# Setup of a patch-pooling transformer tower: biases as a 97th contraction row, weights loaded ahead of the images

## The chip, the cores and the metric

One Trainium2 chip, one of its cores. The metric is the device time of one run in microseconds; the time of a kernel is the median of its runs.

## What is computed

`x` is 64 images x 12 channels x 224 x 224 in fp32. Everything after the first line works on 196 tokens of 192 features per image.

```python
pooled = x.reshape(64, 12, 14, 16, 14, 16).sum(axis=(3, 5))          # 16 x 16 patches
h = einsum('bcij,ce->bije', pooled, channel_weights).reshape(64, 196, 192)
q, k, v = split(layernorm(h) @ W_qkv + b_qkv)                         # W_qkv [192, 576]
h = h + softmax(q @ k.T / sqrt(192)) @ v
C = sum over 9 (e, r) of alpha_e * alpha_r * (mask_out(r*e) x mask_in(e))  # [768, 192]
hid = gelu(layernorm(h) @ (w_fc * C).T + b_fc * c0b)                  # w_fc [768, 192]
out = h + hid @ (w_proj * C.T).T + b_proj * c1b
```

## The kernel before

Every token of the first stage is a combination of 12 channel sums, so the kernel keeps tokens in a basis of at most 26 rows and folds the weights into small matrices once, in a **setup**: `sel_gram` (variance of the first norm), `score_mat` (q and k in one matrix), the basis and its centred transpose `basis_t`, `g2` (variance of the second norm), `resid` (the residual's rows), `f_rows` (w_fc in the basis) and `w1_hi`, `w1_lo` (w_proj in two fp32r parts). Then 16 **groups** of 4 images are worked through in a software pipeline.

*Image loads.* A group is 3 tiles of 128 partitions; a tile is 7 runs of 448 KB, each a DMA of its own on SyncE's (SP's) queue. `xs` holds 2 tiles (RING). VectorE sums a tile in 3 chunks of 2, 2 and 3 runs (`reduce_chunk(n, c)`, L385; c is 0 to 8 within group n). The load of a chunk waits until the chunk two tiles earlier is summed: `sp.wait_ge(reduced, PER_TILE * (tile - RING) + chunk + 1)`. So chunk (0,6), the first of tile 2, waits for sum (0,0), (0,7) for (0,1), (0,8) for (0,2), and (1,0) for (0,3).

*Order.* Each engine runs its program in order. In the groups, tables written by hand (`PE_ORDER`, `DVE_ORDER` ...) give each operation a step; they are not changed. The setup stands ahead of them. On TensorE it is one function: rows of the channel weights, Gram rows, q and k (`PE_QKT`), the score matrix (`PE_A`), coefficients (`PE_COEF`), w_fc turned (`PE_W0T`), basis and residual rows in one signal (`PE_BASIS`), the centred basis turned (`PE_BT`), g2's products, f's products, w_proj turned (`PE_W1`). `sum_rows(0)`, the first product of group 0, comes behind all of it. On VectorE the steps alternate with the first chunk sums:

```python
setup_centre(); setup_mix(); setup_gram()
reduce_chunk(0, 0); setup_scores()
reduce_chunk(0, 1); setup_biases()
reduce_chunk(0, 2); setup_basis()
reduce_chunk(0, 3); setup_g2()
```

*Biases.* q and k's, v's and w_fc's biases are added by products of their own with one contraction row: a bias row of 1 partition against a row of `cr` that has ones where wanted. For w_fc's, TensorE makes the sums c0b with two 384-wide products of 9 rows and VectorE multiplies them into `bfc_sb` in `setup_biases`. An fp32 product is two weight loads and two matmul instructions in the trace, all at line 510 (the helper `mm`); 96 is half of the 192 features (E2).

Of the kernel before, what the change touches and what calls it, by code (L numbers as in the profile page):

```python
# [163 lines left out]
def build(nc, x, cw, wqkv, bqkv, wfc, bfc, wproj, bproj, alpha_e, alpha_r, const_full, const_rows, const_paired, out):  # L164
    with ExitStack() as ctx:
# [208 lines left out]
        def _(dve):  # L374
# [75 lines left out]
            def setup_scores():  # L450
                dve.wait_ge(setup_pe, PE_A)
                dve.tensor_tensor(score_mat[:], ps[:, 1, 0:128], cf[:, MASK_S:MASK_S + 128],
                                  ALU.mult).then_inc(setup_dve, 1)

            def setup_biases():
                dve.wait_ge(setup_pe, PE_W0T)
                dve.wait_ge(wfc_landed, 32)
# [50 lines left out]
        def _(pe):  # L508
# [503 lines left out]
```

## Time and profile before

| | us |
|---|---|
| median of 3 runs | 511.71 (511.31 to 513.15) |
| profiled execution, its own time | 510.34 |
| its span, first to last instruction | 508.2 |
| busy: TensorE products / VectorE / ScalarE / GpSimd | 449.9 / 382.3 / 284.4 / 253.3 |
| first product of group 0 (`sum_rows`) starts | 58.28 |
| last chunk sum starts | 438.38 |

The granted TensorE clock is full (2.4 GHz level) throughout. 166.66 MB are moved, 156.29 of them read. In the trace, PE is TensorE, DVE VectorE, ACT ScalarE, POOL GpSimd, SPq SyncE's DMA queue. A busy share tells how full an engine is, not what sets the end; for that the waits and the order in time have to be read.

### The profile page before, as it was taken

Reading aid. Unit: us, or ns where it says so; the run is one execution under the profiler, and the core shown is the slowest. Engines: PE = TensorE matmul, PEld = TensorE weight load, DVE = VectorE, ACT = ScalarE, POOL = GpSimd, SP = SyncE. Lnnn points to the kernel's source line nnn. Section 1 sums busy time; section 2 is a strip of 40 time slices with the busy share of each in tenths; the row PEclk is TensorE's granted clock in tenths of the full one; section 3 lists DMA queues with packets and bytes.
Section 4 is the critical chain, followed back from the end, with each engine's and each line's share of the span. In section 5 each row is a group of like instructions: output and inputs, shape, how many; then the busy total and the mean of one; then the engine's idle time right before and its main releaser. Section 6 shows DMA issues by size and latency. Waiting matters only on the chain.

```text
span 508.2 us, 11125 instructions
## 1 busy us (share of the span) xinstructions
PE 449.9 (89%) x4676; PEld 374.7 (74%) x4676; DVE 382.3 (75%) x289; ACT 284.4 (56%) x461; POOL 253.3 (50%) x180
## 2 busy tenths in 40 slices
PE   4988563769999999999999999999999998999996
PEld 4644341448888888888888888888788887888886
DVE  2136979999798989898989898989899998710000
ACT  1020210363767676757575757576757575768551
POOL 1022301156283838383747474747474737475570
PEclk9999999999999999999999999999999999999999
DMA  8955999999999999999999999999999999300101
GB/s 243 347 231 194 357 390 366 395 374 397 350 372 393 401 404 401 400 401 401 401 405 401 402 400 400 403 399 400 401 400 397 402 402 390 120 25 26 49 25 49
DMA packets 56652, 166.66 MB, mean 328 GB/s; under 512 B 5967, under 2 KB 13020, under 8 KB 56602
## 3 DMA queue, kind: packets, MB, share of 16 engines
q1 hardware_dynamic: 56602, 165.95, 85.8%
q8 instruction: 37, 0.61, 0.5%
q14 instruction: 13, 0.11, 0.1%
HBM read 156.29 MB, written 9.63 MB: 326 GB/s over the span
## 4 chain that ended last, share of the span: by engine, by line
PE 48%; POOL 22%; issue 12%; ACT 8%; DVE 6%; DMA 3%; SPq 1%; POOLq 0%; ACTq 0%; DVEq 0%
PE ps L510 46%; POOL h_lo L974 10%; POOL inv L953 5%; POOL inv L965 5%; DVE pooled L385 5%; ACT h_hi L885 2%; ACT h_f L876 2%; ACT L876 2%; DMA xs<-x 2%; POOL uhat_tok L967 2%; PE ps L707 1%; POOL phat_tok L958 1%; DMA alpha_sb<-alpha_r 1%; DVE neg_tok L403 0%; ACT out_sb L891 0%
## 5 line engine op out<-in xcount | busy, mean ns | idle before, releaser
L385 DVE TENSOR_REDUCE pooled<-xs 128x28 f32<-128x1792 f32 x144 | 327.5, 2321 | 6.5 <-DMA xs<-x 6.0
L974 POOL TENSOR_TENSOR h_lo<-h_f,h_hi 128x784 fp32r<-128x784 f32 x96 | 176.4, 1866 | 125.4 <-ACT h_hi L885 125.4
L510 PE MATMUL ps<-w_hi,h_hi 128*98 128x192 f32 x768 | 205.4, 267 | 0.0
L510 PE MATMUL ps<-w_lo,h_hi 128*98 128x192 f32 x768 | 194.5, 253 | 0.0
L510 PE MATMUL ps<-w_hi,h_lo 128*98 128x192 f32 x768 | 193.9, 252 | 0.0
L510 PEld LDWEIGHTS ps<-w_hi,h_hi 128*98 128x98 f32 x768 | 126.3, 164 | 18.8 <-issue 15.5
L510 PEld LDWEIGHTS ps<-w_lo,h_hi 128*98 128x98 f32 x768 | 126.7, 165 | 0.0
L510 PEld LDWEIGHTS ps<-w_hi,h_lo 128*98 128x98 f32 x768 | 126.5, 165 | 0.0
L876 ACT ACTIVATE h_f<-ps 128x784 f32<-128x784 f32 x96 | 75.9, 825 | 20.0 <-PE ps L510 19.8
L885 ACT CAST h_hi<-h_f 128x784 fp32r<-128x784 f32 x96 | 81.7, 854 | 0.5
L953 POOL TENSOR_TENSOR inv<-var,minus_half 98x8 f32<-98x8 f32 x16 | 26.2, 1636 | 61.5 <-DVE var L399 61.5
L891 ACT COPY out_sb<-ps 98x384 f32<-98x384 f32 x64 | 30.7, 480 | 33.6 <-PE ps L510 33.1
L510 PE MATMUL ps<-rows_sb,f_rows 32*128 32x196 f32 x768 | 47.6, 364 | 1.7 <-ACT probs L847 1.7
L843 ACT COPY rows_sb<-ps 128x196 f32<-128x196 f32 x16 | 5.2, 322 | 61.5 <-PE ps L510 61.5
L403 DVE TENSOR_REDUCE neg_tok<-ps 98x4 f32<-98x784 f32 x32 | 29.7, 970 | 12.3 <-PE ps L510 12.3
L510 PEld LDWEIGHTS ps<-rows_sb,f_rows 32*128 32x128 f32 x768 | 32.5, 192 | 7.5 <-issue 2.7
L510 PE MATMUL ps<-rows_sb 32*98 32x196 f32 x512 | 33.1, 377 | 1.2 <-ACT rows_sb L843 0.8
L510 PE MATMUL ps<-resid,rows_sb 32*98 32x192 f32 x256 | 28.1, 338 | 1.5 <-ACT out_sb L891 1.5
L847 ACT ACTIVATE probs<-ps 98x784 f32<-98x784 f32 x32 | 24.6, 822 | 3.7 <-PE ps L510 3.5
L965 POOL TENSOR_TENSOR inv<-var,minus_half 98x8 f32<-98x8 f32 x16 | 26.2, 1641 | 0.6 <-DVE var L424 0.6
L510 PEld LDWEIGHTS ps<-rows_sb 32*98 32x98 f32 x512 | 21.2, 176 | 5.9 <-ACT rows_sb L843 1.3
L510 PEld LDWEIGHTS ps<-resid,rows_sb 32*98 32x98 f32 x256 | 20.1, 163 | 6.6 <-issue 4.4
(127 smaller groups left out, 386.3 us busy)
## 6 DMA issues: line engine op xcount, KB each, us to landing
xs<-x SPq DMA_DIRECT2D x336, 448.0 KB, 9.8
out<-out_sb SPq DMA_DIRECT2D x32, 294.0 KB
rows_sb<-wfc SPq DMA_DIRECT2D x1, 576.0 KB
out_sb<-wproj SPq DMA_DIRECT2D x1, 576.0 KB
h_f<-wqkv SPq DMA_DIRECT2D x1, 432.0 KB
cf<-const_full SPq DMA_DIRECT2D x1, 264.0 KB, 4.7
h_f<-const_paired SPq DMA_DIRECT2D x1, 153.0 KB, 5.8
cr<-const_rows SPq DMA_DIRECT2D x1, 83.2 KB
```

Of the source, the lines that this page charges most:

```text
L385: dve.tensor_reduce(pooled[:, n % 2, t, GRID * first:GRID * end].rearrange("p (i j) -> p i j", j=GRID), runs, AX.XY, ALU.add).then_inc(red ...
L403: dve.tensor_reduce(neg_tok[:, :, 2 * pair:2 * pair + 2, NEG].rearrange("p h b -> p b h"), ps[0:HALF, 2 * pair:2 * pair + 2, 0:2 * TOKENS] ...
L510: return pe.matmul(o, a, b, start=start, stop=stop, skip_group_check=shared)
L843: act.copy(phat_neg, ps[:, MB, 0:TOKENS]).then_inc(phat_neg_ready, 1)
L847: act.activation(probs[:, 2 * pair:2 * pair + 2], ps[0:HALF, 2 * pair:2 * pair + 2, 0:2 * TOKENS], ACT.Exp).then_inc(probs_ready, 1)
L876: act.activation(h_f32[:, t].rearrange("p (b n) -> p b n", b=GROUP), ps[:, 0:GROUP, TOKENS * (t % 2):TOKENS * (t % 2 + 1)], ACT.Gelu_apprx ...
L885: act.copy(h_hi[:, m % 2, t], h_f32[:, t]).then_inc(h_hi_ready, 1)
L891: act.copy(out_sb[:, b // 2, b % 2], ps[0:HALF, OB + b % 2, 0:2 * EMBED]).then_inc(out_ready, 1)
L953: pool.tensor_tensor(inv1[:], var1[:], minus_half[:], ALU.pow).then_inc(inv1_ready, 1)
L965: pool.tensor_tensor(inv2[:], var2[:], minus_half[:], ALU.pow).then_inc(inv2_ready, 1)
L967: pool.tensor_tensor(uhat_tok[:, :, :, 0:BASIS].rearrange("p h b c -> p (h b) c"), u_tok[:, m % 2, :, :, 0:BASIS].rearrange("p h b c -> p ...
L974: pool.tensor_tensor(h_lo[:, m % 2, t], h_f32[:, t], h_hi[:, m % 2, t].bitcast(F32), ALU.subtract).then_inc(h_lo_ready, 1)
```

## The change

Bias rows become row 97 (partition 96) of the first half of a contraction that has 96: b_qkv behind `wqkv_sb`, b_fc behind `w0t`, and in the stationary or moving partner a row of constants, brought there by five loads of 512 bytes (`row`). The coefficients get a 97th output row, so b_fc is multiplied together with w_fc on GpSimd, in two halves. The bias products disappear, but for b_proj's. SyncE's queue brings all constants, wqkv and wfc first, then the rows and the alphas, then images. On TensorE the basis is made right behind the score matrix and apart from the residual rows, the coefficients behind it, the centred basis and g2 ahead of w_fc, the residual rows behind it; the places in PSUM follow. On VectorE the steps get another order between the same chunk sums. Sizes of the tiles change with `E2B = E2 + 1`. Shown are declarations, loads and VectorE with what is removed, TensorE, ScalarE and GpSimd with the new lines only (the removed ones are printed above).

```diff
-mix_in = sb("mix_in", [MIXES, EMBED])
-cwt = sb("cwt", [E2, 2, 128])
-cwt_ctx = sb("cwt_ctx", [E2, 2, 128])
+mix_in = sb("mix_in", [MIXES, 2, E2B])
+cwt = sb("cwt", [E2B, 2, 128])
+cwt_ctx = sb("cwt_ctx", [E2B, 2, 128])
-qkt = sb("qkt", [E2, 4, 128])
+qkt = sb("qkt", [E2B, 4, 128])
-basis_t = sb("basis_t", [E2, 2, 128])
+basis_t = sb("basis_t", [E2B, 2, 128])
...
+    def row(out, at):
+        sp.dma_start(out, const_rows[0:1, at:at + 128]).then_inc(rows_landed, 16)
     sp.dma_start(cr[:], const_rows).then_inc(cr_landed, 16)
     sp.dma_start(cw_sb[:], cw).then_inc(cw_landed, 16)
-    for i in range(2):
-        load(0, 0, i)
     sp.dma_start(cf[:], const_full).then_inc(cf_landed, 16)
     sp.dma_start(paired_sb, const_paired).then_inc(cf_landed, 16)
+    sp.dma_start(wqkv_sb[0:E2], wqkv.rearrange("(k p) n -> p k n", k=2)).then_inc(wqkv_landed, 16)
+    sp.dma_start(wqkv_sb[E2:E2B, 0], bqkv).then_inc(wqkv_landed, 16)
+    sp.dma_start(wfc_sb, wfc.rearrange("(t p) e -> p t e", p=128)).then_inc(wfc_landed, 16)
+    row(cwt[E2:E2B, 0], ROW_ONE_P)
+    row(cwt_ctx[E2:E2B, 0], ROW_ONE_U)
+    row(qkt[E2:E2B, 2], ROW_ONE_P)
+    row(qkt[E2:E2B, 0], ROW_NEG)
+    row(basis_t[E2:E2B, 0], ROW_ONE_F)
     sp.dma_start(alpha_sb[:, 0:1], alpha_e).then_inc(mix_landed, 16)
     sp.dma_start(alpha_sb[:, 1:2], alpha_r).then_inc(mix_landed, 16)
-    sp.dma_start(bqkv_sb[:], bqkv).then_inc(wqkv_landed, 16)
-    sp.dma_start(wqkv_sb, wqkv.rearrange("(k p) n -> p k n", k=2)).then_inc(wqkv_landed, 16)
-    for i in range(2, 5):
+    for i in range(4):
         load(0, 0, i)
-    sp.dma_start(bfc_sb[:], bfc).then_inc(wfc_landed, 16)
-    sp.dma_start(wfc_sb, wfc.rearrange("(t p) e -> p t e", p=128)).then_inc(wfc_landed, 16)
-    for i in range(5, RUNS):
+    sp.dma_start(w0t[E2:E2B, 0], bfc).then_inc(bfc_landed, 16)
+    sp.dma_start(bproj_sb[:], bproj).then_inc(bproj_landed, 16)
+    for i in range(4, RUNS):
         load(0, 0, i)
-    sp.dma_start(bproj_sb[:], bproj).then_inc(wproj_landed, 16)
     sp.dma_start(wproj_sb, wproj.rearrange("(k p) h -> p k h", k=2)).then_inc(wproj_landed, 16)
     for i in range(RUNS):
...
-        dve.tensor_scalar(mix_in[:], cr[0:MIXES, ROW_IN:ROW_IN + EMBED], mix[:], None,
-                          ALU.mult).then_inc(setup_dve, 1)
+        dve.tensor_copy(mix_in[:, :, E2:E2B], mix[:].unsqueeze(2).broadcast_to([MIXES, 2, 1]))
+        dve.tensor_scalar(mix_in[:, :, 0:E2], cr[0:MIXES, ROW_IN:ROW_IN + EMBED].rearrange(
+            "p (k e) -> p k e", k=2), mix[:], None, ALU.mult).then_inc(setup_dve, 1)
...
-    def setup_biases():
-        dve.wait_ge(setup_pe, PE_W0T)
-        dve.wait_ge(wfc_landed, 32)
-        dve.wait_ge(wproj_landed, 32)
-        for k in range(2):
-            dve.tensor_tensor(bfc_sb[0:1, 384 * k:384 * (k + 1)], bfc_sb[0:1, 384 * k:384 * (k + 1)],
-                              ps[0:1, 4 + k, 0:384], ALU.mult)
-        dve.tensor_tensor(bproj_sb[:], bproj_sb[:], ps[0:1, 6, 0:EMBED], ALU.mult).then_inc(setup_dve, 1)
...
+    def setup_bias():
+        dve.wait_ge(setup_pe, PE_COEF)
+        dve.wait_ge(bproj_landed, 16)
+        dve.tensor_tensor(bproj_sb[:], bproj_sb[:], ps[0:1, 4, 0:EMBED], ALU.mult).then_inc(setup_dve, 1)
+    def setup_resid():
+        dve.wait_ge(setup_pe, PE_RESID)
+        dve.tensor_copy(resid[:], ps[:, 5, 0:EMBED]).then_inc(setup_dve, 1)
...
     setup_gram()
     reduce_chunk(0, 0)
     setup_scores()
+    setup_basis()
     reduce_chunk(0, 1)
-    setup_biases()
+    setup_g2()
+    setup_bias()
     reduce_chunk(0, 2)
-    setup_basis()
+    setup_resid()
     reduce_chunk(0, 3)
-    setup_g2()
...
+        pe.wait_ge(rows_landed, 16 * BIAS_ROWS)
         for j in range(4):
             o = ps[0:E2, 3, 128 * j:128 * (j + 1)]
+            mm(o, wqkv_sb[:, 0, E2 * j:E2 * (j + 1)], cwt[:, 0, :], True, False)
+            last = mm(o, wqkv_sb[0:E2, 1, E2 * j:E2 * (j + 1)], cwt[0:E2, 1, :], False, True)
         last.then_inc(setup_pe, 1)
         pe.wait_ge(setup_act, ACT_QKT)
+        mm(ps[:, 1, 256:384], qkt[:, 2, :], qkt[:, 0, :], True, False)
+        mm(ps[:, 1, 256:384], qkt[0:E2, 3, :], qkt[0:E2, 1, :], False, True).then_inc(setup_pe, 1)
+        mm(ps[:, 3, 0:EMBED], cr[:, ROW_P:ROW_P + 128], cw_sb[:], True, False)
+        mm(ps[:, 3, 0:EMBED], cwt_ctx[:, 0, :], wqkv_sb[:, 0, 2 * EMBED:3 * EMBED], False, False)
+        mm(ps[:, 3, 0:EMBED], cwt_ctx[0:E2, 1, :], wqkv_sb[0:E2, 1, 2 * EMBED:3 * EMBED], False,
+           True).then_inc(setup_pe, 1)
+        pe.wait_ge(setup_dve, DVE_MIX_IN)
+        mm(ps[0:1, 4, 0:EMBED], mix[:], cr[0:MIXES, ROW_IN:ROW_IN + EMBED])
         for j in range(2):
+            for k in range(2):
+                last = mm(ps[0:E2B, 6 + k if j == 0 else (0, 2)[k], 0:384], mix_in[:, k],
                           cr[0:MIXES, ROW_OUT + 384 * j:ROW_OUT + 384 * (j + 1)])
         last.then_inc(setup_pe, 1)
         pe.wait_ge(setup_dve, DVE_CENTRED)
         for k in range(2):
+            last = pe.transpose(ps[0:E2, 3, 128 * k:128 * (k + 1)], basis_c[:, E2 * k:E2 * (k + 1)], ident)
         last.then_inc(setup_pe, 1)
         pe.wait_ge(setup_act, ACT_BT)
         for k in range(2):
+            last = mm(ps[:, 1, 0:128], basis_t[0:E2, k, :], basis_t[0:E2, k, :], k == 0, k == 1)
         last.then_inc(setup_pe, 1)
+        pe.wait_ge(wfc_landed, 16)
+        pe.wait_ge(setup_act, ACT_COEF)
+        for k in range(2):
+            for t in range(4):
+                pe.transpose(ps[0:E2, 6 + k, 128 * t:128 * (t + 1)], wfc_sb[:, t, E2 * k:E2 * (k + 1)], ident)
+        for k in range(2):
+            for t in range(4, HT):
+                last = pe.transpose(ps[0:E2, 2, 256 * k + 128 * (t - 4):256 * k + 128 * (t - 3)],
+                                    wfc_sb[:, t, E2 * k:E2 * (k + 1)], ident)
+        last.then_inc(setup_pe, 1)
+        pe.wait_ge(setup_dve, DVE_BIAS)
+        o = ps[:, 5, 0:EMBED]
+        mm(o, cr[:, ROW_P:ROW_P + 128], cw_sb[:], True, False)
+        mm(o, cwt_ctx[:, 0, :], wqkv_sb[:, 0, 2 * EMBED:3 * EMBED], False, False)
+        mm(o, cwt_ctx[0:E2, 1, :], wqkv_sb[0:E2, 1, 2 * EMBED:3 * EMBED], False, False)
+        mm(o, cr[0:1, ROW_ONE_U:ROW_ONE_U + 128], bproj_sb[0:1, :], False, True).then_inc(setup_pe, 1)
+        pe.wait_ge(setup_pool, POOL_W0T_1)
+        pe.wait_ge(setup_act, ACT_W0T)
         for j in range(2):
+            o = ps[:, 6 + j, 0:384]
+            mm(o, basis_t[:, 0, :], w0t[:, 0, 384 * j:384 * (j + 1)], True, False)
+            last = mm(o, basis_t[0:E2, 1, :], w0t[0:E2, 1, 384 * j:384 * (j + 1)], False, True)
         last.then_inc(setup_pe, 1)
         pe.wait_ge(setup_pool, POOL_WPROJ)
         for t in range(HT):
             for k in range(2):
                 at = EMBED * (t % 2) + E2 * k
+                last = pe.transpose(ps[:, (0, 2, 3)[t // 2], at:at + E2], wproj_sb[:, k, 128 * t:128 * (t + 1)],
                                     ident[0:E2, 0:E2])
         last.then_inc(setup_pe, 1)
...
         act.wait_ge(setup_pe, PE_COEF)
+        act.copy(coef[:, :, 0:384], ps[0:E2B, 6:8, 0:384])
+        act.copy(coef[:, 0, 384:768], ps[0:E2B, 0, 0:384])
+        act.copy(coef[:, 1, 384:768], ps[0:E2B, 2, 0:384]).then_inc(setup_act, 1)
+        act.wait_ge(setup_pe, PE_BT)
+        act.copy(basis_t[0:E2], ps[0:E2, 3, 0:256].rearrange("p (k c) -> p k c", k=2)).then_inc(setup_act, 1)
         act.wait_ge(setup_pe, PE_W0T)
+        act.copy(w0t[0:E2, :, 0:512], ps[0:E2, 6:8, :])
+        act.copy(w0t[0:E2, :, 512:768],
+                 ps[0:E2, 2, :].rearrange("p (k c) -> p k c", k=2)).then_inc(setup_act, 1)
         act.wait_ge(setup_pe, PE_F)
+        act.copy(f_rows[:].rearrange("p (k c) -> p k c", k=2), ps[:, 6:8, 0:384]).then_inc(setup_act, 1)
         act.wait_ge(setup_pe, PE_W1)
+        for bank, at in ((0, 0), (2, 2), (3, 4)):
+            act.copy(w1_hi[:, at:at + 2, :], ps[:, bank, 0:384].rearrange("p (t e) -> p t e", t=2))
+        for bank, at in ((0, 0), (2, 2), (3, 4)):
+            last = act.copy(w1_f32[:, at:at + 2, :], ps[:, bank, 0:384].rearrange("p (t e) -> p t e", t=2))
+        last.then_inc(setup_act, 1)
...
+        pool.wait_ge(bfc_landed, 16)
+        pool.tensor_tensor(w0t[:, 0], w0t[:, 0], coef[:, 0], ALU.mult).then_inc(setup_pool, 1)
+        pool.tensor_tensor(w0t[0:E2, 1], w0t[0:E2, 1], coef[0:E2, 1], ALU.mult).then_inc(setup_pool, 1)
+        pool.wait_ge(wproj_landed, 16)
+        pool.tensor_tensor(wproj_sb, wproj_sb, coef[0:E2], ALU.mult).then_inc(setup_pool, 1)
         pool.wait_ge(setup_act, ACT_W1)
```

## Rows read from the trace of the kernel before

**Rows 1.** Windows by stage: busy time (instructions) per engine, clock, DMA share, GB/s

```profile
58.00:150.00 92.00, 65.89 (x561) 50.32 (x562) 82.33 (x61) 38.47 (x68) 37.38 (x27) 1.00 1.00 380
150.00:330.00 180.00, 172.63 (x2048) 150.71 (x2046) 169.18 (x122) 124.93 (x201) 107.08 (x71) 1.00 1.03 401
330.00:430.00 100.00, 93.65 (x1110) 81.32 (x1110) 91.63 (x67) 67.85 (x110) 60.35 (x40) 1.00 1.03 400
```

**Rows 2.** Waits of VectorE, 320 to 430 us: total, times, longest

```profile
DVE pooled L385 <- DMA xs<-x: 4.4, 9, 0.8
```

**Rows 3.** Timeline at the last chunk sum: start, duration, idle before

```profile
438.38 2.95 DVE L385 TENSOR_REDUCE pooled<-xs 128x42 f32<-128x2688 f32 x1 [0.69 <-DMA xs<-x]
...
441.48 0.73 PE L510 MATMUL ps<-sel_gram,pooled 128*98 128x96 f32 x6 [0.25 <-DVE pooled L385]
```

**Rows 4.** Windows over the setup, transfers in the last two columns

```profile
22.00:32.40 10.40, 10.40 (x25) 4.30 (x25) 2.22 (x2) 1.49 (x2) 0.00 (x0) 1.00 1.03 404
32.40:39.00 6.60, 5.02 (x15) 3.35 (x13) 4.13 (x4) 1.49 (x2) 3.89 (x2) 1.00 0.08 20
39.00:43.00 4.00, 3.32 (x9) 2.28 (x8) 0.62 (x2) 0.00 (x0) 2.92 (x1) 1.00 0.92 320
43.00:47.20 4.20, 2.77 (x8) 1.93 (x9) 3.61 (x6) 0.37 (x1) 0.00 (x0) 1.00 0.05 19
47.20:58.00 10.80, 9.79 (x23) 4.40 (x21) 10.80 (x5) 1.77 (x3) 0.00 (x0) 1.00 0.95 309
```

**Rows 5.** Timeline of VectorE, 9 to 62 us

```profile
22.54 2.01 DVE L385 TENSOR_REDUCE pooled<-xs 128x28 f32<-128x1792 f32 x1
...
34.66 2.93 DVE L385 TENSOR_REDUCE pooled<-xs 128x42 f32<-128x2688 f32 x1
42.36 0.36 DVE L466 COPY resid<-ps 128x192 f32<-128x192 f32 x1 [4.76 <-PE ps L510]
...
43.83 2.01 DVE L385 TENSOR_REDUCE pooled<-xs 128x28 f32<-128x1792 f32 x1
...
60.26 0.26 DVE L399 TENSOR_REDUCE var<-prod 98x8 f32<-98x104 f32 x1
```

**Rows 6.** Chain of waits, 0 to 62 us: start, length, what

```profile
4.38 4.66 DMA alpha_sb<-alpha_r
...
9.87 9.83 PE ps L510 x36
...
30.70 1.87 PE ps L565 x8
...
35.01 7.33 PE ps L510 x18
```

**Rows 7.** Windows over the first loads

```profile
4.00:7.00 3.00, 2.52 (x12) 2.31 (x12) 0.31 (x1) 0.00 (x0) 0.00 (x0) 1.00 1.03 388
7.00:10.00 3.00, 0.80 (x6) 0.53 (x5) 0.90 (x5) 0.78 (x3) 0.00 (x0) 1.00 1.05 212
13.00:15.00 2.00, 2.00 (x9) 1.45 (x8) 0.00 (x0) 0.00 (x0) 0.00 (x0) 1.00 1.09 348
```

**Rows 8.** Timeline of TensorE: weight loads (PEld), products (PE)

```profile
12.55 1.17 PE L510 MATMUL ps<-cwt,h_f 96*96 96x128 f32 x4
...
13.64 0.39 PEld L510 LDWEIGHTS ps<-cr,bqkv_sb 1*96 1x96 f32 x2 [0.28 <-issue]
...
20.35 1.22 PE L510 MATMUL ps<-qkt 96*128 96x128 f32 x4 [0.67 <-ACT qkt L799]
...
22.09 5.32 PE L510 MATMUL ps<-cr,mix_in 9*96 9x384 f32 x8
```

**Rows 9.** Timeline of ScalarE and GpSimd in the setup

```profile
27.45 0.79 ACT L801 COPY probs<-ps 96x768 f32<-96x768 f32 x1 [7.15 <-PE ps L510]
...
35.11 3.42 POOL L945 TENSOR_TENSOR h_f<-h_f,probs 96x1536 f32<-96x1536 f32 x1 [32.17 <-ACT h_f L805]
...
61.95 1.64 POOL L953 TENSOR_TENSOR inv<-var,minus_half 98x8 f32<-98x8 f32 x1
```

More of the change, by code:

```diff
@@ L543, in setup @@
                 last.then_inc(setup_pe, 1)
                 pe.wait_ge(setup_act, ACT_QKT)
-                for j in range(2):
-                    mm(ps[:, 1, 0:128], qkt[:, 2 + j, :], qkt[:, j, :], j == 0, False)
-                mm(ps[:, 1, 0:128], cr[0:1, ROW_ONE_P:ROW_ONE_P + 128], cr[0:1, ROW_NEG:ROW_NEG + 128], False,
+                mm(ps[:, 1, 256:384], qkt[:, 2, :], qkt[:, 0, :], True, False)
+                mm(ps[:, 1, 256:384], qkt[0:E2, 3, :], qkt[0:E2, 1, :], False, True).then_inc(setup_pe, 1)
@@ L549, in setup @@
+                mm(ps[:, 3, 0:EMBED], cr[:, ROW_P:ROW_P + 128], cw_sb[:], True, False)
+                mm(ps[:, 3, 0:EMBED], cwt_ctx[:, 0, :], wqkv_sb[:, 0, 2 * EMBED:3 * EMBED], False, False)
+                mm(ps[:, 3, 0:EMBED], cwt_ctx[0:E2, 1, :], wqkv_sb[0:E2, 1, 2 * EMBED:3 * EMBED], False,
                    True).then_inc(setup_pe, 1)
                 pe.wait_ge(setup_dve, DVE_MIX_IN)
-                for k in range(2):
-                    for j in range(2):
-                        last = mm(ps[0:E2, 2 + k if j == 0 else 6 + k, 0:384], mix_in[:, E2 * k:E2 * (k + 1)],
+                mm(ps[0:1, 4, 0:EMBED], mix[:], cr[0:MIXES, ROW_IN:ROW_IN + EMBED])
@@ L555, in setup @@
+                for j in range(2):
+                    for k in range(2):
+                        last = mm(ps[0:E2B, 6 + k if j == 0 else (0, 2)[k], 0:384], mix_in[:, k],
                                   cr[0:MIXES, ROW_OUT + 384 * j:ROW_OUT + 384 * (j + 1)])
-                last.then_inc(setup_pe, 1)
-                for j in range(2):
-                    mm(ps[0:1, 4 + j, 0:384], mix[:], cr[0:MIXES, ROW_OUT + 384 * j:ROW_OUT + 384 * (j + 1)])
-                pe.wait_ge(setup_act, ACT_COEF)
@@ L560, in setup @@
-                mm(ps[0:1, 6, 0:EMBED], mix[:], cr[0:MIXES, ROW_IN:ROW_IN + EMBED])
-                pe.wait_ge(wfc_landed, 32)
-                for k in range(2):
-                    for t in range(4):
-                        pe.transpose(ps[0:E2, 2 + k, 128 * t:128 * (t + 1)], wfc_sb[:, t, E2 * k:E2 * (k + 1)], ident)
-                for k in range(2):
-                    for t in range(4, HT):
-                        last = pe.transpose(ps[0:E2, 7, 256 * k + 128 * (t - 4):256 * k + 128 * (t - 3)],
-                                            wfc_sb[:, t, E2 * k:E2 * (k + 1)], ident)
@@ L570, in setup @@
-                last.then_inc(setup_pe, 1)
-                pe.wait_ge(setup_act, ACT_W0T)
-                pe.wait_ge(setup_dve, DVE_BIAS)
-                for at in (0, 256):
-                    o = ps[:, 3, at:at + EMBED]
-                    mm(o, cr[:, ROW_P:ROW_P + 128], cw_sb[:], True, False)
-                    for k in range(2):
-                        mm(o, cwt_ctx[:, k, :], wqkv_sb[:, k, 2 * EMBED:3 * EMBED], False, False)
-                    last = mm(o, cr[0:1, ROW_ONE_U:ROW_ONE_U + 128], bqkv_sb[0:1, 2 * EMBED:3 * EMBED], False, at == 0)
-                    if at:
-                        last = mm(o, cr[0:1, ROW_ONE_U:ROW_ONE_U + 128], bproj_sb[0:1, :], False, True)
@@ L585, in setup @@
                 for k in range(2):
-                    last = pe.transpose(ps[0:E2, 2, 128 * k:128 * (k + 1)], basis_c[:, E2 * k:E2 * (k + 1)], ident)
+                    last = pe.transpose(ps[0:E2, 3, 128 * k:128 * (k + 1)], basis_c[:, E2 * k:E2 * (k + 1)], ident)
                 last.then_inc(setup_pe, 1)
@@ L589, in setup @@
                 for k in range(2):
-                    last = mm(ps[:, 1, 0:128], basis_t[:, k, :], basis_t[:, k, :], k == 0, k == 1)
+                    last = mm(ps[:, 1, 0:128], basis_t[0:E2, k, :], basis_t[0:E2, k, :], k == 0, k == 1)
                 last.then_inc(setup_pe, 1)
-                pe.wait_ge(setup_pool, POOL_W0T)
+                pe.wait_ge(wfc_landed, 16)
[16 more added lines that the diff above has]
+                pe.wait_ge(setup_act, ACT_W0T)
                 for j in range(2):
-                    o = ps[:, 4 + j, 0:384]
-                    for k in range(2):
-                        mm(o, basis_t[:, k, :], w0t[:, k, 384 * j:384 * (j + 1)], k == 0, False)
-                    last = mm(o, cr[0:1, ROW_ONE_F:ROW_ONE_F + 128], bfc_sb[0:1, 384 * j:384 * (j + 1)], False, True)
+                    o = ps[:, 6 + j, 0:384]
+                    mm(o, basis_t[:, 0, :], w0t[:, 0, 384 * j:384 * (j + 1)], True, False)
+                    last = mm(o, basis_t[0:E2, 1, :], w0t[0:E2, 1, 384 * j:384 * (j + 1)], False, True)
                 last.then_inc(setup_pe, 1)
@@ L804, in setup @@
-                act.copy(w0t[:, :, 0:512], ps[0:E2, 2:4, :])
-                act.copy(w0t[:, :, 512:768],
-                         ps[0:E2, 7, :].rearrange("p (k c) -> p k c", k=2)).then_inc(setup_act, 1)
-                act.wait_ge(setup_pe, PE_BT)
-                act.copy(basis_t[:], ps[0:E2, 2, 0:256].rearrange("p (k c) -> p k c", k=2)).then_inc(setup_act, 1)
+                act.copy(coef[:, :, 0:384], ps[0:E2B, 6:8, 0:384])
+                act.copy(coef[:, 0, 384:768], ps[0:E2B, 0, 0:384])
```

51 lines of the change are left out of this document (19 added, 32 removed).

## Prediction

> **What bounds the kernel now.** I read the end first and went backwards. In the windows by stage [rows 1] the transfer engines are busy without a gap (share 1.03) from 150 us on, at 400 to 401 GB/s, while TensorE is busy for 94 to 96% and VectorE for 92 to 94% of the time. Three resources are almost equally full, so the question is which one is late at the end. VectorE's waits from 320 to 430 us [rows 2] say which: nine times it waits for an image run that has not landed, 4.4 us in all. The last chunk sum shows it again [rows 3]: VectorE idles 0.69 us for the transfer, starts at 438.38 and takes 2.95 us, and TensorE starts sum_rows of the last group at 441.48 after waiting for it. What follows, 508.2 - 441.3 = 66.9 us, is the drain of the last two groups, and the change does not touch it. So the end is the last landing plus a fixed tail. The last landing is the time for the bytes plus the time in which the transfer engines have nothing to do. That idle time lies in the setup [rows 4]: they work at 404 GB/s up to 32.4 us, then have almost nothing until 39, work until 43, and have nothing again until 47.2. The two holes are 6.6 and 4.2 us, 10.8 together, plus a thinner stretch (309 GB/s) to 58 us.
>
> The holes are made by VectorE's program order. The load of a chunk of tile 2 or 3 waits for the sum of the same chunk two tiles earlier. VectorE sums (0,1) at 22.54, (0,2) at 34.66 and (0,3) at 43.83 [rows 5], each queued behind a setup step that waits for TensorE; data for all of them is there long before. Transfers restart 1.4 us after a sum ends: 34.66 + 2.93 = 37.6, first bytes at 39; 43.83 + 2.01 = 45.8, first bytes at 47.2. From (0,3) on the sums run back to back. The start of (0,3) is therefore the number that the change has to move.
>
> **The change, in the order of the path.** *Loads.* The alphas now queue behind the weights instead of behind two image runs. Before, they landed at 9.04 [rows 6]. Leaving out two runs (0.92 MB, at 388 GB/s) saves 2.4 us; putting in wqkv (0.44 MB at 212 GB/s, the rate of the stretch that holds the narrow constants and wqkv) and wfc (0.59 MB at 348) adds 2.1 + 1.7 us [rows 7]. Net +1.4 us, so the alphas land at 10.4. SP is not what they wait for: alpha_r was its eighth load, issued at 4.38, and becomes the fourteenth, at the same pace at most at 4.38 x 14/8 = 7.7 us. The extra broadcast copy into mix_in is one more tiny VectorE step, 0.1 us. The Gram rows on TensorE, which began at 9.87 [rows 6], start at 11.35 (+1.5). Bounds: landing between 9.0 (no later than before) and 13.5 (wfc too at 212 GB/s or worse, and each small load with some delay of its own), that is -1.4 to +3 us. The five row loads land with the alphas and are wanted only at 14 us. The first image chunk now lands near 13, 3 us later, and costs nothing: its sum is followed by a wait for score_mat until 20 us, a cover of 5 us.
>
> *q and k.* A group of four instructions with 96 rows takes 1.09 us to the next weight load, and each one-row bias group behind it costs the rest of the pitch, with 0.28 us of pure waiting at the change of height [rows 8]. Sixteen instructions without the bias ones take 4 x 1.09 = 4.4 us: from 14.05 to 18.5, where the old end was 9.87 + 9.83 = 19.7 [rows 6]. Whether 97 rows cost more than 96 no row shows. The nearest, weight loads and products with 12, 9 or 1 rows against 96, hardly differ, so I take nothing; the upper bound is the same 0.28 us at each alternation of 97 and 96.
>
> *A, then the basis.* The copy (0.67 us of TensorE's idling) and four instructions (1.22 us [rows 8]) end at 20.4 instead of 22.3. The basis no longer waits for the coefficients, the weight transposes and both biases. It is six instructions at 7.33/18 = 0.41 us [rows 6], 2.5 us, done at 22.9 where it was done at 42.3 [rows 5]. VectorE centres it in 1.3 us and sums (0,1) from 24.1, 1.6 us **later** than before. That is free: the transfers queued by then last to 32.4, or 30.1 without the two runs that (0,1) releases, and (0,1) would have to end after 28.6 to open a hole. It ends at 26.1.
>
> *Coefficients, centred basis, g2.* The narrow proj-bias product (0.7 us with its change of height) and eight of 5.32 us [rows 8] follow: 29.1, against 27.4. The two wide coefficient products for bfc and their VectorE multiplications are gone. ScalarE copies in three pieces, 1.55 us for 1.5 (the first 0.79 [rows 9]), then basis_t, 0.4: 31.05. The G2 products (the same shape as A's four, 1.22) end at 32.3; g2 and the one bias product on VectorE take 0.6. **Sum (0,2) starts at 32.9 instead of 34.66.** TensorE waits for ScalarE about 1.3 us here, which is in the sum.
>
> *Weight transposes, residual row.* Twelve transposes at 1.87/8 [rows 6] take 2.8 us: 35.1. The residual set, eight instructions at 0.41 and a change of height, 3.4 us: 38.5. VectorE copies it in 0.35. **Sum (0,3) starts at 38.85 instead of 43.83, 5.0 us earlier.** Holes after: 32.4 to 35.8 + 1.4 = 37.2, then 4.0 us of transfer, and 41.2 to 40.85 + 1.4 = 42.25; 4.8 + 1.05 = 5.85 us instead of 10.8. Both ways of counting give 5.0.
>
> *What is off the path.* GpSimd's product in two halves costs the same 3.42 us [rows 9] and 0.1: 36.65 to 40.2. The f products, eight at 0.67, end at 45.5, the last twelve transposes by 48.3 (2.8 again at most). Group 0's sum_rows needs VectorE's chunk (0,8), whose end is 38.85 + 4 x 2.0 + 2 x 2.9 = 52.7 at the earliest. So TensorE has 4.4 us of cover; if that were gone, each us late there delays group 0 but not the loads. ScalarE's six W1 copies (half the width of the 0.79 one, 0.4 each, 2.4) and GpSimd's w1_lo (1152 columns against 1536, 2.6) end at 53.3. Before, the variance was there at 60.5 [rows 5] and w1_lo made the first power wait until 61.95 [rows 9]; now it starts with its variance, near 55.5, 6.4 us earlier. Group 0's chain thus gains 1.4 us more than the loads. VectorE's later stops for TensorE become a little shorter against the landings, and part of the 1.00 instead of 1.03 busy share between 58 and 150 us [rows 1] comes back: at least 0, at most 0.03 x 92 = 2.8 us; I take 0.5, since most of that dip also has low GB/s at full share, which no earlier issue mends.
>
> **Sum.** 5.0 + 0.5 = 5.5 us. The profiled span goes from 508.2 to 502.7, its own time from 510.34 to 504.8. The median of the runs stands 1.37 us above that profiled time, so 511.71 becomes **506.2**.
>
> **The rivals.** *Larger* (chance 0.12): the chain's lead of 6.4 us and nearly all of the 2.8 us come back, 5.0 + 2.8 = 7.8, or about 8.2 with part of the thin stretch before 58 us; 503.5. Against it: the share is already 1.03 over most of that stretch. *Small, no measurable change* (0.14): mixed heights of 97 and 96 are a change like 96 to 1. Before (0,3) there are eleven in q, k, A and the basis and three in the residual set: 14 x 0.28 = 3.9 us, a gain of 1.6, 510.1. Late alphas (+3 us) end at 2.5, in the same place. The Trainium skill (TensorEngine Tiling (Array Packing), Key Properties) says that a change of tiling mode drains the engine, and its configurations have 32, 64 or 128 rows. By that rule 97 and 96 share a mode and this rival would be void; the pause at 96 to 1 agrees with the first half, and no row here shows the second. *Slower* (0.06): the small loads are served one after the other. If each of the five row loads held the alphas up by 2 us, under half of the 4.66 us that alpha_r took from issue to landing [rows 6], 10 us go onto the path before the Gram rows; 511.71 - 5.5 + 10 = 516.2. It decides from alphas landing at 10.4 + 5.5 = 15.9 on. Against it, alpha_r landed at 9.04 with seven loads ahead of it, two of them whole image runs: hardly more than 1 us for each of the eight, bytes included. The Trainium skill (DMA: Bandwidth & Descriptors, Rules for kernel authors) puts small transfers down as mostly overhead and wants them merged; with its fixed 2 us for each of five, unoverlapped, the result would be this rival's. That the end were led by TensorE's chain and not by the loads is no rival for the sign: that chain moves by 6.4 us as well.
>
> **How the numbers follow.** The forecast has 0.68. With the larger case 0.80 is faster by over 0.5% (2.6 us, about what a measurement of this kernel can tell from no change), 0.14 within it, 0.06 slower. The range runs from the larger case with 0.8 us for the scatter of the runs, 502.7, to a gain of 2.2 us, 509.5, which takes in most of the late-alpha bound.
>
> **What would show it.** Alphas: VectorE's mix starts at 10.4. Heights: the q and k products take 4.4 us and show no pause between 97 and 96. Basis: sum (0,1) at 24.1; (0,2) at 32.9; (0,3) at 38.85. Loads: two holes of 4.8 and 1.05 us. Late chain: the first power at 55.5. End: the last chunk sum starts near 432.9, still after a wait for its run, and 66.9 us follow its end. The prediction is wrong if (0,3) does not come 3 to 7 us earlier, if a new hole opens after 50 us, if the stretch from 150 us on has a lower GB/s, or if the last sum no longer waits for its run.

## The result and the profile after

The changed kernel takes **497.61 us** (median of 4 runs, 497.16 to 498.95) against 511.51 for the kernel before beside it: ratio 0.9731, 95% interval 0.9703 to 0.976. The gain is 13.9 us where 5.5 was forecast, and the time is below the range. The profiled executions compare at 510.34 before and 498.95 after, with spans of 508.2 and 496.8. So their difference, 11.4 us, is what the traces explain. The other 2.5 us are where these two executions lie among the runs: the one of before is below the median of its runs, the one of after is the longest of its four. Two disturbed executions of later runs, 794.96 us in e5 and 609.01 us in e8, are left out of every number below.

I read the setup first. VectorE's timeline of the kernel after (start, duration, what ended the idle time before) is to be laid beside [rows 5]:

```profile
10.44 0.15 DVE L446 TENSOR_TENSOR mix<-alpha_sb 9x1 f32<-9x1 f32 x1 [6.11 <-DMA alpha_sb<-alpha_r]
...
23.37 2.01 DVE L395 TENSOR_REDUCE pooled<-xs 128x28 f32<-128x1792 f32 x1
31.86 2.93 DVE L395 TENSOR_REDUCE pooled<-xs 128x42 f32<-128x2688 f32 x1
37.39 0.36 DVE L484 COPY resid<-ps 128x192 f32<-128x192 f32 x1 [2.61 <-PE ps L522]
37.67 15.43 DVE L395 TENSOR_REDUCE pooled<-xs 128x28 f32<-128x1792 f32 x7
53.30 0.26 DVE L409 TENSOR_REDUCE var<-prod 98x8 f32<-98x104 f32 x1
```

The alphas land as forecast (10.44). The sums (0,1), (0,2) and (0,3) start at 23.37, 31.86 and 37.67, and group 0's variance stands at 53.3. GpSimd's first power follows at once:

```profile
53.64 1.65 POOL L964 TENSOR_TENSOR inv<-var,minus_half 98x8 f32<-98x8 f32 x1 [2.11 <-DVE var L409]
```

Before, it started at 61.95 [rows 9]: 8.3 us. TensorE's timeline of after shows q and k without a pause, 3.73 us for sixteen instructions of two heights (eight with 97 rows and eight with 96, in turn):

```profile
11.31 2.75 PE L522 MATMUL ps<-gram,h_f 48*128 48x24 f32 x12 [2.79 <-DVE gram L459]
14.00 3.73 PE L522 MATMUL ps<-cwt,h_f 97*96 97x128 f32 x16
18.39 1.22 PE L522 MATMUL ps<-qkt 97*128 97x128 f32 x4 [0.67 <-ACT qkt L807]
```

The windows of after (window, length, then PE, PEld, DVE, ACT and POOL busy, granted clock, DMA share, GB/s) show the two holes in the loads and the stages behind them, where [rows 1, 4] stand for before:

```profile
22.00:31.60 9.60, 8.28 (x20) 3.82 (x20) 3.33 (x7) 1.83 (x4) 0.00 (x0) 1.00 1.01 410
31.60:36.20 4.60, 4.60 (x17) 3.44 (x15) 3.19 (x3) 1.49 (x2) 0.62 (x1) 1.00 0.07 23
36.20:40.50 4.30, 2.46 (x5) 1.33 (x5) 3.11 (x3) 0.00 (x0) 4.30 (x3) 1.00 0.90 309
40.50:41.50 1.00, 1.00 (x3) 0.56 (x2) 1.00 (x1) 0.00 (x0) 1.00 (x1) 1.00 0.65 100
150.00:330.00 180.00, 172.53 (x2041) 150.48 (x2040) 168.65 (x123) 125.42 (x202) 109.38 (x72) 1.00 1.03 409
330.00:415.00 85.00, 80.83 (x956) 70.39 (x955) 80.02 (x61) 58.42 (x97) 53.14 (x37) 1.00 1.03 409
```

The holes are of about the forecast size. But the steady stretch moves **409 GB/s instead of 401**, in the same share of busy time. That was not forecast, and it changes what ends the kernel. VectorE's waits from 320 to 430 us now hold no run of images (us in all, times, longest us, as in [rows 2]):

```profile
DVE row_inv L421 <- PE ps L695: 6.0, 5, 1.2
DVE neg_tok L413 <- PE ps L522: 1.0, 4, 0.3
```

Its timeline at the end shows the last chunk sum starting without a wait, where [rows 3] had one of 0.69 us:

```profile
426.26 0.21 DVE L421 RECIPROCAL row_inv<-ps 98x8 f32<-98x8 f32 x1 [1.21 <-PE ps L695]
426.51 0.26 DVE L423 TENSOR_TENSOR u_tok<-ps,row_inv 98x96 f32<-98x96 f32 x1
426.68 2.94 DVE L395 TENSOR_REDUCE pooled<-xs 128x42 f32<-128x2688 f32 x1
```

From its end, 429.6, to the span's end are 67.2 us, against the 66.9 forecast. The groups' maxima tell where the 11.4 us arise. These are VectorE's rows of the kernel before and then of the kernel after, for groups 3, 10 and 15 (the last):

```profile
145.48 1.86 DVE L403 TENSOR_REDUCE neg_tok<-ps 98x4 f32<-98x784 f32 x2 [0.25 <-PE ps L510]
...
320.93 1.86 DVE L403 TENSOR_REDUCE neg_tok<-ps 98x4 f32<-98x784 f32 x2 [0.25 <-PE ps L510]
...
448.77 1.86 DVE L403 TENSOR_REDUCE neg_tok<-ps 98x4 f32<-98x784 f32 x2 [5.03 <-PE ps L510]
```

```profile
136.86 1.86 DVE L413 TENSOR_REDUCE neg_tok<-ps 98x4 f32<-98x784 f32 x2 [0.26 <-PE ps L522]
...
312.33 1.86 DVE L413 TENSOR_REDUCE neg_tok<-ps 98x4 f32<-98x784 f32 x2 [0.25 <-PE ps L522]
...
437.38 1.86 DVE L413 TENSOR_REDUCE neg_tok<-ps 98x4 f32<-98x784 f32 x2 [5.04 <-PE ps L522]
```

The lead is 8.6 us at group 3, still 8.6 at group 10, and 11.4 at the end. From group 3 to group 10 the groups of both kernels come every 25.07 us, and VectorE of the kernel before has no wait for a run between 150 and 320 us. Only then do the loads of the kernel before fall behind: its next groups come after 25.7, 26.1, 25.4 and 25.9 us, those of the kernel after still after 25.1. These stops make the 2.8 us. Two questions were left: where the 409 GB/s come from, and which part of the change gives the 8.6 us.

### The profile page after: what moved, and what is told of

Read it like the earlier page. It is cut to its first block, busy times and chain, and to the rows that moved or that the text cites. A ratio compares the mean times of both kernels' runs of the same rounds, so it can differ in the third digit from the quotient of the medians.

```text
span 496.8 us, 11091 instructions
## 1 busy us (share of the span) xinstructions
PE 438.0 (88%) x4654; PEld 370.2 (75%) x4654; DVE 380.4 (77%) x288; ACT 284.7 (57%) x464; POOL 253.6 (51%) x181
## 4 chain that ended last, share of the span: by engine, by line
PE 48%; POOL 23%; issue 12%; ACT 8%; DVE 5%; DMA 3%; SPq 1%; POOLq 0%; ACTq 0%; DVEq 0%
PE ps L522 46%; POOL h_lo L985 10%; POOL inv L964 5%; POOL inv L976 5%; DVE pooled L395 4%; ACT h_hi L894 2%; ACT h_f L885 2%; ACT L885 2%; POOL uhat_tok L978 2%; DMA xs<-x 2%; PE ps L715 1%; POOL phat_tok L969 1%; DMA alpha_sb<-alpha_r 1%; DVE neg_tok L413 0%; ACT out_sb L900 0%
## 5 line engine op out<-in xcount | busy, mean ns | idle before, releaser
L421 DVE RECIPROCAL row_inv<-ps 98x8 f32<-98x8 f32 x16 | 3.3, 207 | 29.7 <-PE ps L695 29.7
```

## The experiments

The runs were measured at three times, and the kernel before beside them took 511.0 us (e1 to e4), 513.33 (e5 to e8) and 512.98 (e9 to e11). Between runs of different times the ratios to it are therefore the safer measure, and times that differ by under a microsecond are not told apart.

**Where the rate comes from.** One thing differs for every image load: where its buffer lies. xs started at byte 55264 of a partition, 224 beyond a multiple of 256, and now starts at 49920, a multiple of 256. bqkv_sb and bfc_sb lay ahead of it and are gone, but they had 2304 and 3072 bytes of each partition, 9 and 12 times 256, and so did not change the start modulo 256. What changed it is mix_in, whose rows grew from 192 to 194 floats: it starts 5376 bytes lower than before (28128 instead of 33504), and the buffers behind it only 5344. Each run writes 3584 bytes, 14 x 256, to each partition. Theory A: the start of xs modulo 256 sets the rate. Theory B: the rate follows from the new timing of the setup. Two kernels cross the address with the rest of the change, by padding ahead of xs and behind it:

```diff
 e1, in the kernel before            e2, in the kernel after
+sb("pad_a", [128, 8])              +sb("pad_a", [128, 56])
 xs = sb("xs", ...)                  xs = sb("xs", ...)
+sb("pad_b", [128, 56])             +sb("pad_b", [128, 8])
```

> The kernel before, with 32 bytes of padding ahead of the image ring xs and 224 behind it. xs starts at byte 55264 of a partition before the change (224 behind a multiple of 256) and at 49920 after it (a multiple of 256), because the bias buffers ahead of it are gone; here it starts at 55296, a multiple of 256. Theory A (the address sets the rate of the image loads): from 150 us on the loads keep up, about 408 to 410 GB/s as in the changed kernel instead of 401, VectorE has no waits for runs after 320 us, and the time falls from 511.5 to between 506 and 508.7. Theory B (the rate follows from the order of the setup or the phase between the engines): 511.5, 401 GB/s, nothing changes.

> The changed kernel, with 224 bytes of padding ahead of xs and 32 behind it, so that xs has the offset of the kernel before again (224 behind a multiple of 256). Theory A: 401 GB/s, VectorE waits for runs in the later groups, and only the shorter setup is left of the gain: 502 to 505.5. Theory B: 497.6, 409 GB/s.

The kernel before with an aligned xs took 507.63 us (506.34 to 509.07, 10 runs; before 511.0), ratio 0.9923, interval 0.9897 to 0.9949. The changed kernel with the old offset took 500.92 (499.29 to 502.11, 6 runs), ratio 0.9793 (0.9755 to 0.9831). The windows of e1, then of e2:

```profile
150.00:330.00 180.00, 172.59 (x2044) 150.73 (x2043) 169.18 (x122) 124.78 (x200) 108.57 (x72) 1.00 1.03 409
```

```profile
150.00:330.00 180.00, 172.52 (x2041) 150.49 (x2040) 168.34 (x123) 125.21 (x202) 108.95 (x72) 1.00 1.03 402
```

The rate goes with the address and not with the setup; nor does it go with the granted clock, whose mean is 0.99 in e1's profile and 0.935 in those of e2 and of the kernel after. So do the stops: e1 has none for images after 150 us, and e2 has them again, as its waits of VectorE from 150 to 430 us show:

```profile
DVE pooled L397 <- DMA xs<-x: 6.2, 10, 1.4
```

Theory A holds. The four kernels are nearly additive: the address is worth 3.3 to 3.4 us in either setup (511.0 - 507.6; 500.9 - 497.6), and the rest of the change 10.0 to 10.1 (507.6 - 497.6; 511.0 - 500.9). The intervals of the two ratios reach 1.3 us (e1) and 1.9 us (e2) to either side.

**Which offsets cost.** The padding ahead of xs was set to 16, 8 and 32 floats in the kernel after, which gives offsets of 64, 32 and 128 bytes.

> The changed kernel with 64 bytes of padding ahead of xs (and 192 behind it). The last two runs showed that xs 224 behind a multiple of 256 costs both kernels 3.3 to 3.4 us. Which step of the address counts is open. Theory A (a multiple of 64 is enough): 409 GB/s from 150 us on and 497.6. Theory B (it must be a multiple of 256): 402 GB/s and 500.9.

> The changed kernel with 32 bytes of padding ahead of xs (and 224 behind it). Theory A (a multiple of 64 is wanted) and theory B (a multiple of 256): both 402 GB/s and 500.9. Theory C (only an offset as far as 224 hurts, say by a run's end that spills over): 409 GB/s and 497.6.

> The changed kernel with 128 bytes of padding ahead of xs and 128 behind. So far: a multiple of 256 gives 409 to 410 GB/s from 150 to 330 us and no wait of VectorE for a run, 64 behind it 405 and 4.6 us of waits, 32 and 224 behind it 401 and 402. Theory A (each run's rows are cut at multiples of 256, so every offset costs an extra piece, and offsets that are no multiple of 64 cost more): 405 GB/s, waits of a few us, 498 to 500. Theory B (a multiple of 128 is as good as one of 256): 409 and no waits, 497.6.

Mean rate from 150 to 330 us, VectorE's waits for images from 150 us on (total and times), median time from issue to landing of a run, and the time:

| xs modulo 256 | GB/s | waits, us | landing, us | time, us (ratio) |
|---|---|---|---|---|
| 0, after | 409 | none | 7.3 | 497.61 (0.9731) |
| 128, e10 | 407 | none | 8.6 | 497.25 (0.971) |
| 64, e5 | 405 | 4.6 / 9 | 9.5 | 499.04 (0.9756) |
| 32, e6 | 401 | 3.8 / 6 | 9.8 | 501.65 (0.9794) |
| 224, e2 | 402 | 6.2 / 10 | 10.2 | 500.92 (0.9793) |

A group moves 10.236 MB, 9.634 of images in and 0.602 of results out, and has a period of 25.07 us: 408 GB/s. So 409 is what is asked for, and 401 and 402 fall short by 0.4 to 0.5 us a group, which is why the stops come only in the later groups. The times of 64, 32 and 224 are not told apart (their intervals overlap), but the landing times are in order. The theories that a multiple of 64 is enough, and that only an offset as far as 224 hurts, are refuted by the waits of e5 and e6; at 128 the runs are nearer to theory B of e10. The Trainium skill (DMA: Bandwidth & Descriptors, How a descriptor splits into AXI transactions) says, of reads, that transactions start at 256-byte boundaries. Applied to the written side, which is an estimate from that page, it would make 15 of an unaligned piece of 3584 bytes instead of 14, the same number at each offset. The runs agree that a multiple of 256 is best, but not that the others are equal: 128 costs almost nothing in time.

**Where the 8.6 us arise: the loads.** With the loads off the path, theory A is that the end follows the setup's chain alone, alphas, steps, group 0's first power. Theory B is that the loads still set it. e3 lets the alphas go first; e4 restores the loads' old order, two image runs ahead of alphas and weights.

```diff
 e3
+sp.dma_start(alpha_sb[:, 0:1], alpha_e).then_inc(mix_landed, 16)   # behind cw
+sp.dma_start(alpha_sb[:, 1:2], alpha_r).then_inc(mix_landed, 16)
 sp.dma_start(wqkv_sb[0:E2], wqkv.rearrange("(k p) n -> p k n", k=2)).then_inc(wqkv_landed, 16)
...
-sp.dma_start(alpha_sb[:, 0:1], alpha_e).then_inc(mix_landed, 16)
-sp.dma_start(alpha_sb[:, 1:2], alpha_r).then_inc(mix_landed, 16)
```

> The changed kernel with the two alpha loads moved from behind the five rows to right behind cw. Theory A (TensorE's setup chain starts with VectorE's wait for the alphas, 10.44 us): mix starts before 5 us, the Gram rows at 8.7 to 10 us instead of 11.31, and the whole chain comes 1.3 to 2.6 us earlier: 495.0 to 496.3. Theory B (the setup is hidden behind the image loads by now): 497.6 within 0.5.

> The changed kernel with the kernel before's order of loads: two image runs ahead of the constants, alphas behind those, wqkv, three runs, wfc, two runs, wproj; the five rows behind the alphas. Theory A (putting the weights ahead costs 1.4 us at the alphas and gains nothing, since no step waited for a weight before): mix at 9.1 instead of 10.44, 496.2. Theory B (the order of the loads is part of the gain): 499 or more.

e3 took 494.7 (494.6 to 495.09), ratio 0.9676 (0.9635 to 0.9718). Mix starts at 4.23, sum (0,3) at 33.62, the first power at 49.59: 4.05 us earlier, where at most 2.6 were expected. The span is 4.2 us shorter and the time 2.9. e4 took 495.47 (494.86 to 497.29), ratio 0.9695 (0.9656 to 0.9734); its mix starts at 8.80 and its maxima 1.64 us earlier. Both follow theory A in the mechanism, and both times are below its numbers. Weights ahead of images is thus the part of the change that costs: 1.6 us by e4's trace and 2.1 by its time, for nothing.

**The row of biases.** e7 puts the one-row products of q and k, the score matrix, the basis and the residual rows back; b_fc stays row 97:

```diff
-mm(o, wqkv_sb[:, 0, E2 * j:E2 * (j + 1)], cwt[:, 0, :], True, False)
-last = mm(o, wqkv_sb[0:E2, 1, E2 * j:E2 * (j + 1)], cwt[0:E2, 1, :], False, True)
+for k in range(2):
+    mm(o, wqkv_sb[0:E2, k, E2 * j:E2 * (j + 1)], cwt[0:E2, k, :], k == 0, False)
+last = mm(o, bqkv_sb[0:1, E2 * j:E2 * (j + 1)], cr[0:1, ROW_ONE_P:ROW_ONE_P + 128], False, True)
...
```

> The changed kernel with the one-row bias products of q and k, the score matrix, the basis and the residual rows put back in place of row 97 (b_qkv in a buffer of its own, 9 x 256 bytes, so that xs stays at a multiple of 256); b_fc stays row 97, the order stays new. Theory A (the setup's gain is mostly the missing one-row products: the 16 instructions of q and k took 3.73 us where 24 took 7.15): the score matrix 4.2 us later, sum (0,3) near 43.4 instead of 37.67, end 503.3. Theory B (it is mostly the order): below 500.

It took 502.88 (502.12 to 503.9), ratio 0.981 (0.9765 to 0.9856). (0,1) starts at 27.92, (0,3) at 42.86 instead of 37.67, the variance at 58.49 instead of 53.30. The q and k rows of e7 have the pitch of [rows 8] again:

```profile
13.78 1.17 PE L523 MATMUL ps<-cwt,h_f 96*96 96x128 f32 x4
14.88 0.74 PE L523 MATMUL ps<-cr,bqkv_sb 1*96 1x128 f32 x2
15.54 1.17 PE L523 MATMUL ps<-cwt,h_f 96*96 96x128 f32 x4
```

So the 97th row gives 5.2 us of the setup, more than half of the lead, as theory A had it (503.3 us).

**The order of the steps.** e8 keeps all but the order: coefficients, weight transposes and biases again ahead of the basis.

```diff
-PE_A, PE_BASIS, PE_COEF, PE_BT, PE_G2, PE_W0T, PE_RESID, PE_F, PE_W1
+PE_A, PE_COEF, PE_W0T, PE_BASIS, PE_RESID, PE_BT, PE_G2, PE_F, PE_W1
...
```

> The changed kernel with the kernel before's order of steps on TensorE, ScalarE and VectorE (coefficients, w_fc turned, then basis and residual rows, then the centred basis and g2; biases between sums (0,1) and (0,2), basis ahead of (0,3), g2 behind it); row 97 and the order of the loads stay new. Theory A (row 97 carries the gain): (0,1) near 20 and (0,2) near 26 come earlier than in the changed kernel, (0,3) near 37.4 as there, g2 behind it costs 0.7: 498.3. Theory B (the order is worth as much as the rows): 501 or more.

It took 500.92 us (500.29 to 501.28), ratio 0.9775 (0.973 to 0.982); span 498.1, 1.3 us longer than in the changed kernel. (0,1) starts at 19.14, (0,2) at 25.29, (0,3) at 38.13, g2 only at 40.65, and the variance at 54.56. That is 1.3 us later than in the changed kernel although its mix started 0.7 earlier, so the order is worth about 2 us. The time is near theory B's, the steps are near theory A's. 0.7 us are the wait for g2, which stands behind (0,3), as A had it. Another 1.2 was expected by neither theory, and without it (0,3) would come 27.2 us behind the mix, just as in the changed kernel. VectorE's centring of the basis took 1.50 us instead of 0.32, beside GpSimd's product of w_proj:

```profile
34.68 3.42 POOL L958 TENSOR_TENSOR out_sb<-out_sb,probs 96x1536 f32<-96x1536 f32 x1
36.71 1.50 DVE L475 TENSOR_SCALAR h_f<-h_f,basis_mean 128x192 f32<-128x192 f32 x1
```

The two end together (38.10 and 38.21). In the kernel before the same step ran at 43.59, when GpSimd had nothing to do, and took 0.32. The Trainium skill (GPSIMD Engine Reference, Specifications) says that GpSimd shares its interfaces to SBUF with VectorE, and that they contend where VectorE's instruction is in a two-port mode or reads two inputs from SBUF. The trace agrees that a step can be slowed; it is one instruction of one run, and which condition it met is not shown.

**Better versions.** e9 adds to e3 that VectorE sums chunks as early as their data are there. e11 adds that GpSimd makes w1_lo behind group 0's first scale instead of ahead of its first power.

```diff
 e9, VectorE's setup order
+reduce_chunk(0, 1)    # ahead of the scores
-reduce_chunk(0, 1)
+reduce_chunk(0, 2)    # behind the centred basis
+reduce_chunk(0, 3)
-reduce_chunk(0, 2)
+reduce_chunk(0, 4)    # behind g2 and the bias
-reduce_chunk(0, 3)
 e11, GpSimd
-pool.wait_ge(setup_act, ACT_W1)
-pool.tensor_tensor(w1_lo[:], w1_f32, w1_hi[:].bitcast(F32), ALU.subtract).then_inc(setup_pool, 1)
...
+if m == 0: (the same two statements, behind scale_p)
```

> The kernel with the alphas first (494.7 us), and on VectorE the chunk sums put where their data are there and VectorE waits for TensorE: (0,1) ahead of score_mat, (0,2) and (0,3) behind the basis, (0,4) between the biases and the residual copy. Theory A (the end follows group 0's first power, which w1_lo on GpSimd then holds back: it ends at 48.1 where the variance came at 49.5): 1.4 us, 493.3. Theory B (the end follows the holes in the loads, which close by several us more): 491 or less. Theory C (the setup is no longer on the path): 494.7.

> The same as the run with the early sums, and GpSimd makes w1_lo behind group 0's power and scaling instead of ahead of them. Theory A: the first power starts with its variance near 46.0 instead of 49.6 with the alphas alone, 3.6 us earlier: 491.1. Theory B and C: as the run before, no difference between the two.

e9 took 493.75 (493.23 to 494.49), ratio 0.9644 (0.9606 to 0.9683). It shuts the holes: the busy share of the loads from 22 to 50 us goes from 0.93 in e3 to 1.01. It gains 0.95 us over e3 in time, 1.3 in span and 0.8 at the first power. That is nearer to theory A (493.3) than to B (491 or less), though a gain of this size is near the scatter of the times. What holds its first power is not the data but w1_lo:

```profile
46.23 2.62 POOL L961 TENSOR_TENSOR w_lo<-h_f,w_hi 128x1152 fp32r<-128x1152 f32 x1 [6.23 <-ACT h_f L825]
48.80 1.65 POOL L965 TENSOR_TENSOR inv<-var,minus_half 98x8 f32<-98x8 f32 x1
```

In e11 the power waits for its variance alone:

```profile
47.38 1.64 POOL L963 TENSOR_TENSOR inv<-var,minus_half 98x8 f32<-98x8 f32 x1 [7.26 <-DVE var L409]
49.40 2.62 POOL L995 TENSOR_TENSOR w_lo<-h_f,w_hi 128x1152 fp32r<-128x1152 f32 x1
```

It took **492.21** (491.4 to 492.71), ratio 0.9608 (0.957 to 0.9647), the best of all. Its first power is at 47.38 where 46.0 was expected (491.1 us). Its maxima come 1.42 us earlier than those of e9 at group 0, and 0.95 at the last group.

## Why the prediction was wrong

The sign and most steps of the setup were right. **The step that failed is "the end is the last landing plus a fixed tail", with the rate of the loads taken as unchanged.** The sum asked what each edit does to time and nothing about where it leaves the buffers. The eight bytes that mix_in grew by moved xs to a multiple of 256 bytes. The loads then keep pace with VectorE, and the end follows the chain of VectorE, TensorE and GpSimd, whose groups come every 25.07 us in both kernels wherever no run is late. This is shown by e1 and e2 and is worth 3.3 to 3.4 us. With the loads off the path, the number that counts is the chain's lead. The prediction had it, at 6.4 us, and threw it away as "1.4 us more than the loads". Even of the kernel before the step held only for the last five groups: [rows 2] stand for 320 to 430 us, and between 150 and 320 us VectorE had no such wait.

The rate is not the whole miss. With the old address the time is 500.92 us (e2), still below the range. Of the 8.4 us by which the gain of 13.9 exceeds the forecast 5.5, 3.2 are the spans' difference between e2 and the kernel after (500.0 - 496.8). 2.7 are a lead of the loads that was forecast too small: 8.2 us (508.2 - 500.0) instead of 5.5. The last 2.5 are the place of the two profiled executions among their runs.

*The loads' lead, 5.5 forecast, 8.2 measured with the old address.* The two terms of the sum were near, and the thin stretch was put at nothing. The mean rates of the kernel before and of e2, and what the difference is worth at 401 GB/s:

| stretch, us | before, GB/s | e2, GB/s | worth, us | forecast, us |
|---|---|---|---|---|
| 0 to 22 | 278 | 292 | 0.8 | none |
| 22 to 50, the holes | 236 | 306 | 4.9 | 5.0 |
| 50 to 58 | 303 | 401 | 2.0 | none |
| 58 to 150, the dip | 380 | 383 | 0.7 | 0.5 |

So the thin stretch before 58 us, which the prediction read in [rows 4] and left out of the sum, came back nearly whole, while the dip behind it stayed. The rival *larger* named 8.2 us as well, but from nearly all of the dip's 2.8 and a part of the thin stretch; that its number agrees is luck.

*The chain's lead, 6.4 forecast, 8.3 measured at the first power (8.6 from group 1 on).* A term mis-sized, in two places. (0,3) came 6.16 us earlier and not 5.0: q and k took 3.73 us and not 4.4, which is about the 0.7 us by which (0,1) was ahead of its forecast 24.1, and G2 and its copy were done 1.0 us before the forecast 32.9 for (0,2). And "from (0,3) on the sums run back to back" did not hold for before: g2 stood behind (0,3) and waited for TensorE, so that the next sum began at 46.55, 0.7 us after the end of (0,3); the changed order saves that.

*Right.* The alphas at 10.4 (10.44). The Gram rows at 11.35 (11.31). (0,1) later than before at no cost. Holes of 4.8 and 1.05 us (4.6, and 1.0 in which the loads are not quite idle). Residual row, f products and GpSimd's halves off the path: the first power waits 2.1 us for its variance. The tail.

*The rivals.* *Small* is void: 97 and 96 rows alternate without a pause, and the late alphas stayed at +1.4. The Trainium skill (TensorEngine Tiling (Array Packing), Key Properties) says that a change of tiling mode drains the engine; by it 97 and 96 rows share a mode, and the trace agrees. *Slower* is void: the five row loads are issued 0.3 to 0.4 us apart, from 3.70 us on, and the alphas behind them are there at 10.44 and not at 15.9. The Trainium skill (DMA: Bandwidth & Descriptors, Rules for kernel authors) calls transfers this small mostly overhead; the 2 us for each that the rival charged did not add up here.

*Open.* Why offsets of 128, 64 and 32 bytes differ as they do; the runs show that they do and not what in the transfer path makes it. Of e3, 1.5 of the 4.05 us have no cause of their own: up to (0,2) it is 2.5 us ahead, and from 31.3 us on its residual products run faster than in the kernel after (four of 97 x 192 in 0.92 us instead of 1.65), and no edit asks for that. Why VectorE's step slows down in e8 is argued from one coincidence.

## What to carry to other kernels

When an edit adds, removes or resizes a buffer, work out again where every later buffer starts: here the two buffers that went left the offset alone, and eight bytes more in a third changed it. A destination of heavy loads belongs at a multiple of 256 bytes, and padding settles it in one line. When two resources are nearly equally full, work out the lead of both chains and let neither be the answer alone; the windows' GB/s against the bytes of a period over its length (here 401 against 408) say which one is short. Read the waits of the whole steady stretch and not of its end alone: the one that is late last may have been on time for most of the run. Small loads that the first step needs go ahead of large ones, and an engine's program order should put nothing that can wait, such as w1_lo, ahead of what the next group waits for.

## What the runs showed of the hardware that was not expected

The start of xs modulo 256, above: 401 to 409 GB/s, and 7.3 to 10.2 us from issue to landing of a run.

VectorE's 128 x 192 tensor_scalar took 1.50 us instead of 0.32 beside GpSimd's product (e8).

The granted clock and the durations do not go together. TensorE idled from 46.4 to 51.3 us in the changed kernel, and then the page's row of the granted clock shows half, the 1.2 GHz level, until 110 us; before stayed at full, the 2.4 GHz level, throughout. This is that row of after's page, one digit for each fortieth of the span:

```profile
PEclk9999555558999999999999999999999999999999
```

No price of it shows: VectorE's waits for the maxima of groups 1 and 2 (1.16 and 1.17 us) and for the first context (3.59) are the same in both kernels. Nor does one show over whole executions. Among the fifteen of the kernel before beside e1, the three with a mean granted clock of 0.913 to 0.919 took 509.13 to 511.0 us, the others, with 0.98 to 1.00, 510.4 to 515.91. And the same four products took 1.17 us in the kernel before at 108 us and 0.60 at 136, both at granted 1.00:

```profile
108.27 1.17 PE L510 MATMUL ps<-g,rows_sb 128*98 128x128 f32 x4
...
136.39 0.60 PE L510 MATMUL ps<-g,rows_sb 128*98 128x128 f32 x4
```

In the kernel after they take 1.17 us in the stretch granted 0.50 too. Only e1 shows a price: a granted 0.76 and 0.73 between 110 and 130 us, and 0.9 us more of VectorE's wait for the context (4.48 instead of 3.59).
